# A two-layer block on one core: the last three token mixes of the second phase in one run on three row strips, and the step orders rewritten

## What is computed

```
xa = _ln(x, ln1_w, ln1_b)
sx = jnp.concatenate([state[:, 1:2] - xa[:, :1], xa[:, :-1] - xa[:, 1:]], axis=1)
xxx = jnp.tanh((xa + sx * maa_x) @ maa_w1).reshape(b, l, 5, DM)
xxx = jnp.einsum('blfd,fde->blfe', xxx, maa_w2)
xm = xa[:, :, None] + sx[:, :, None] * (maa_stack + xxx)
xk, xw, xv, xr, xg = (xm[:, :, j] for j in range(5))
w = jnp.exp(-jnp.exp(time_decay + jnp.tanh(xw @ td_w1) @ td_w2))
r, k, v = xr @ Wr.T, xk @ Wk.T, xv @ Wv.T
g = jax.nn.silu(xg @ Wg.T)
# scan over time, per head: out = r (u * k v + s);  s = k v + w * s
og = group norm of out, per head, * gn_w + gn_b
x1 = x + og * g @ Wo.T
xc = _ln(x1, ln2_w, ln2_b)
sx2 = jnp.concatenate([state[:, 0:1] - xc[:, :1], xc[:, :-1] - xc[:, 1:]], axis=1)
rr = jax.nn.sigmoid((xc + sx2 * ffn_maa_r) @ Wfr.T)
kk = jnp.square(jax.nn.relu((xc + sx2 * ffn_maa_k) @ Wfk.T))
return x1 + rr * (kk @ Wfv.T)
```

## Time and profile before

| what | value |
|---|---|
| time, median of 3 runs | 1576.75 us (1575.3 to 1579.61) |
| the profiled execution: its time, its span | 1575.7 us, 1573.9 us |
| TensorE busy | 1444.3 us, 92% |
| VectorE busy | 929.1 us, 59% |
| ScalarE busy | 719.3 us, 46% |
| GpSimd busy | 469.1 us, 30% |
| mean granted clock of TensorE | 0.967 |

### The profile page before, as it was taken

How to read it: one execution, slowest core, us unless ns; L and a number is a source line. 1 busy time by engine, 2 the same in 40 slices (tenths; PEclk the granted TensorE clock), 3 DMA queues, 4 the chain that set the end, 5 groups by cost and what they waited for, 6 DMA issues and landing times. The chain is left out here.

```text
span 1573.9 us, 33178 instructions
## 1 busy us (share of the span) xinstructions
PE 1444.3 (92%) x12352; PEld 1081.0 (69%) x12352; DVE 929.1 (59%) x2287; ACT 719.3 (46%) x1772; POOL 469.1 (30%) x530
## 2 busy tenths in 40 slices
PE   4999999999999999668899999999999999999965
PEld 4777777777777777366667667666766676767632
DVE  2444444444444443327678787878777877887651
ACT  3666666666666666412433343334433443334312
POOL 1211111111111111024334532453245334533330
PEclk9999999999999999867999999999999999999977
DMA  7431111111111100020000000000000000000000
GB/s 202 146 86 39 38 38 38 37 37 37 37 37 37 37 12 13 18 113 13 18 25 6 20 24 25 9 16 25 24 18 8 24 25 18 8 24 19 18 6 12
DMA packets 25663, 54.59 MB, mean 35 GB/s; under 512 B 3984, under 2 KB 6672, under 8 KB 24016
## 3 DMA queue, kind: packets, MB, share of 16 engines
q1 hardware_dynamic: 25552, 52.99, 11.7%
HBM read 42.23 MB, written 7.34 MB: 31 GB/s over the span
## 5 line engine op out<-in xcount | busy, mean ns | idle before, releaser
L896 POOL TENSOR_TENSOR rst<-rp,st 128x448 f32<-128x448 f32 x192 | 195.2, 1041 | 67.9 <-DVE st L1092 67.9
L268 POOL TENSOR_TENSOR aT_lo<-whole,aT_hi 128x375 fp32r<-128x375 f32 x64 | 58.6, 916 | 450.0 <-ACT whole L420 447.1
L340 DVE CUSTOM_DVE_ANT_0 probs<-a_bank,unmask 112x375 f32<-112x375 f32 x256 | 125.9, 544 | 83.1 <-PE a_bank L537 72.4
L888 POOL TENSOR_TENSOR xm<-mixed,xa 128x448 f32<-128x448 f32 x80 | 84.9, 1077 | 301.7 <-DVE mixed L1021 274.0
L439 ACT ACTIVATE probs<-probs,least 112x375 f32<-112x375 f32 x256 | 153.8, 608 | 0.0
L346 DVE RECIPROCAL inv_rows<-sums 112x128 f32<-112x128 f32 x64 | 61.0, 953 | 156.1 <-ACT probs L439 156.1
L448 ACT COPY probsT<-a_bank 125x448 f32<-125x448 f32 x192 | 90.3, 536 | 53.2 <-PE a_bank L590 53.2
L590 PEld LDWEIGHTS a_bank<-ident_sb,probs 112*125 112x125 f32 x768 | 92.0, 190 | 31.1 <-ACT keyT L430 16.3
L1100 DVE TENSOR_TENSOR rst<-rp,st 128x448 f32<-128x448 f32 x64 | 109.7, 1715 | 0.0
L590 PE MATMUL a_bank<-ident_sb,probs 112*125 112x112 f32 x768 | 100.6, 281 | 3.4 <-ACT probs L439 3.4
L1021 DVE SCALAR_TENSOR_TENSOR mixed<-b_bank,vec_sb,sx 128x112 f32<-128x112 f32 x320 | 83.0, 325 | 31.9 <-PE b_bank L1537 31.6
(11 more groups left out here) (165 smaller groups left out, 3213.5 us busy)
## 6 DMA issues: line engine op xcount, KB each, us to landing
ctx_tok<-in_ctx SPq DMA_DIRECT2D x16, 750.0 KB
xT_sb<-in_xT SPq DMA_DIRECT2D x16, 224.0 KB, 9.7
x_tok<-in_x SPq DMA_DIRECT2D x16, 224.0 KB, 9.2
x_between_layers<-x_sb SPq DMA_DIRECT2D x16, 224.0 KB, 2.3
b_x<-x_between_layers SPq DMA_DIRECT2D x16, 224.0 KB, 2.8
x_post<-x_between_layers SPq DMA_DIRECT2D x16, 224.0 KB, 2.8
out_dram<-fin SPq DMA_DIRECT2D x16, 224.0 KB, 2.3
vbd<-vtok SPq DMA_DIRECT2D x208, 16.0 KB
```

The costliest lines, as they stand in the source:

```text
L340: dve.tensor_tensor_reduce(out=probs[:, g % 2, i], in0=score_bank[i][0:T, 0:TC], in1=unmask[:, m[1]], scale=-SCALE, scalar=-LOWEST, op0=AL ...
L888: pool.tensor_tensor(xm[:, f % 2], mixed[:, f % 2], xa[:, :, 1:T + 1], ALU.add).then_inc(s_xm, 1)
L896: pool.tensor_tensor(by_chunk(rst[:, j % NPROD]), by_chunk(rp[:].rearrange("p c t -> p (c t)")), state_of(j), ALU.mult).then_inc(s_pprod, 1)
```

## The change

The rows of the gate's mix move from strip 0 to strip 1 (row 5 instead of 4), in `maa2`, in `th` and in the output of `maa_first`. Mixes k, r and g then lie on strips 0, 3 and 1 and in banks 2, 1 and 0, and TensorE computes them in one interleaved run of `maa_second`, behind `reduce 0`; before, k ran alone and r with g. The orders of all four engines' steps are rewritten:

- TensorE: `transpose_value` goes behind the gate projection and behind reductions 2 and 3, which move to that place; `reduce 1` goes behind the key projection; `attend_near 3` ahead of `project_out`; `maa_first` ahead of `ffn_receptance`.
- ScalarE: `spread_decay` goes behind the chunk keys; `decay_rate` ahead of `gn_affine`, `copy_value` behind it; `decay_factor` behind `xa_affine`; `copy_vtok` behind `tanh_gate` and `relu_square`. `tanh_gate` also waits for the decay factor now, which reads the buffer that it writes.
- VectorE: `wkv_sum` goes to the head of the step; `stats1` ahead of `finish`; `bonus_value` ahead of mixes 0 and 1; product 3 ahead of `near_values 0`; product 7 right behind mix 2; `near_values 3` and product 15 ahead of `shift2`.
- GpSimd: mix 2 stands between products 5 and 6, mix 3 behind 6, mix 4 ahead of 9, and `xa_state` ahead of 13.

SyncE's steps are as before.

```diff
 MIXES = ["maa_w", "maa_v", "maa_k", "maa_r", "maa_g"]
-MIX_ROW = [1, 2, 0, 3, 4]
+MAA_ORDER = ["maa_k", "maa_w", "maa_v", "maa_r", "maa_g"]
+LAST_ROWS = slice(MD, 2 * MD)
+MIX_ROW = [1, 2, 0, 3, 5]
...
                 act.activation(th[:, 0], pre_bank[1][:, 0:T], ACT.Tanh)
-                act.activation(th[0:MD, 1], pre_bank[1][0:MD, T:2 * T], ACT.Tanh).then_inc(s_th, 1)
+                act.activation(th[LAST_ROWS, 1], pre_bank[1][LAST_ROWS, T:2 * T], ACT.Tanh).then_inc(s_th, 1)
...
                 act.wait_ge(s_gmm, count(b, 1, 1))
+                act.wait_ge(s_wdec, count(b, 1, 1))
...
-                for o, (a, z) in enumerate(((0, P), (P, MAA * MD))):
+                for o, (a, z, rows_of) in enumerate(((0, P, slice(0, P)), (P, MAA * MD, LAST_ROWS))):
...
-                        last = pe.matmul(pre_bank[1][0:z - a, o * T:(o + 1) * T], maa1[:, c, a:z], xin[:, c], start=(c == 0),
+                        last = pe.matmul(pre_bank[1][rows_of, o * T:(o + 1) * T], maa1[:, c, a:z], xin[:, c], start=(c == 0),
...
                     attend_near(m, 1)
-                if pre:
-                    maa_second(n, (2,))
-                if scans:
                     attend_near(m, 2)
                     reduce(m, 0)
                 if pre:
-                    maa_second(n, (3, 4))
+                    maa_second(n, (2, 3, 4))
...
                 if post:
                     transpose_post(l)
                 if pre:
-                    transpose_value(n)
+                    project(n, 4, "wg", s_gmm)
                 if scans:
                     reduce(m, 2)
-                if more:
-                    transpose_x(p)
-                if pre:
-                    project(n, 4, "wg", s_gmm)
+                    reduce(m, 3)
+                if pre:
+                    transpose_value(n)
                 if post:
                     ffn_key(l)
-                    ffn_receptance(l)
                 if more:
                     maa_first(p)
                 if post:
+                    ffn_receptance(l)
                     ffn_value(l)
-                if scans:
-                    reduce(m, 3)
...
                 if pre:
+                    decay_factor(n)
                     copy_rec(n)
+                    tanh_gate(n)
+                if post:
+                    relu_square(l)
+                if pre:
                     copy_vtok(n)
-                    tanh_gate(n)
-                if post:
-                    relu_square(l)
+                if post:
                     receptance(l)
...
+                if post:
+                    wkv_sum(l)
                 if scans:
                     prefixes(m)
                     for d in range(2, CH + 1):
                         decay_key(m, d)
+                    near_products(m, 0)
                     decay_rec(m)
-                    near_products(m, 0)
                     near_products(m, 1)
+                if more:
+                    stats1(p)
                 if post and at_least(n, 3):
                     finish(later(n, -3))
-                if post:
-                    wkv_sum(l)
-                if more:
-                    stats1(p)
+                if scans:
+                    bonus_value(m)
```

More of the change, by code:

```diff
@@ L933, in step @@
                     mix(n, 1)
+                if more:
+                    rstd1(p)
                 if scan:
@@ L940, in step @@
                     gate_output(l, scan)
-                if more:
-                    rstd1(p)
                 if scan:
                     product(m, 5)
+                if pre:
+                    mix(n, 2)
+                if scan:
                     product(m, 6)
                 if pre:
-                    mix(n, 2)
                     mix(n, 3)
@@ L950, in step @@
                     product(m, 8)
-                    product(m, 9)
                 if post:
                     rstd2(l)
-                if scan:
-                    product(m, 10)
                 if pre:
@@ L958, in step @@
                 if scan:
+                    product(m, 9)
+                    product(m, 10)
                     product(m, 12)
+                if more:
+                    xa_state(p)
+                if scan:
                     product(m, 13)
                     product(m, 14)
-                if more:
-                    xa_state(p)
             run(pool, step)
@@ L1199, in step @@
                 if scans:
-                    bonus_value(m)
                     near_products(m, 2)
                     scan(m)
+                    product(m, 3)
                     near_values(m, 0)
-                    product(m, 3)
                 if post:
@@ L1207, in step @@
                 if scans:
+                    near_products(m, 3)
                     near_values(m, 1)
+                if more:
+                    apply1(p)
                 if pre:
@@ L1211, in step @@
                 if scans:
-                    near_products(m, 3)
+                    product(m, 7)
                 if pre:
                     mix(n, 3)
-                if scans:
-                    product(m, 7)
                 if post:
                     residual(l)
+                if pre:
+                    mix(n, 4)
+                if post:
+                    stats2(l)
                 if scans:
                     product(m, 11)
-                if post:
-                    stats2(l)
-                if more:
-                    apply1(p)
-                if pre:
-                    mix(n, 4)
                 if post:
@@ L1230, in step @@
                     near_values(m, 2)
+                    near_values(m, 3)
+                    product(m, 15)
                 if post:
                     shift2(l)
-                if scans:
-                    product(m, 15)
+                if more:
+                    token_shift(p)
                 if post:
@@ L1237, in step @@
                     ffn_input(l, xr2, "ffn_r", s_xr2)
-                if scans:
-                    near_values(m, 3)
+                if more:
+                    mix_input(p)
                 if pre:
                     gate(n)
-                if more:
-                    token_shift(p)
-                    mix_input(p)
                 if is_batch(l, B - 1):
@@ L1435, in step @@
                 if scans:
+                    chunk_keys_decayed(m)
+                    spread_decay(m)
                     copy_keys(m)
@@ L1446, in step @@
                 if pre:
-                    copy_value(n)
+                    decay_rate(n)
                 if post:
@@ L1450, in step @@
                 if pre:
-                    decay_rate(n)
-                    decay_factor(n)
+                    copy_value(n)
                     copy_key(n)
@@ L1458, in step @@
                 if pre:
+                    decay_factor(n)
                     copy_rec(n)
-                    copy_vtok(n)
                     tanh_gate(n)
@@ L1463, in step @@
                     relu_square(l)
+                if pre:
+                    copy_vtok(n)
+                if post:
                     receptance(l)
@@ L1678, in step @@
                 if scans:
+                    bonus(m)
                     transpose_keys(m)
-                    bonus(m)
                 if pre:
@@ L1705, in step @@
                 if pre:
-                    maa_second(n, (3, 4))
+                    maa_second(n, (2, 3, 4))
+                if scans:
+                    attend_near(m, 3)
                 if post:
                     project_out(l)
+                if pre:
+                    project(n, 2, "wk", s_kmm)
                 if scans:
                     reduce(m, 1)
-                    attend_near(m, 3)
                 if pre:
-                    project(n, 2, "wk", s_kmm)
                     project(n, 3, "wr", s_rmm)
+                if more:
+                    transpose_x(p)
                 if post:
```

13 lines of the change are left out of this document (4 added, 9 removed).

## The result

| | kernel before | kernel after |
|---|---|---|
| median of the runs | 1577.97 us (4 runs, 1575.3 to 1579.61) | 1614.51 us (4 runs, 1612.97 to 1618.83) |
| profiled execution: time, span | 1575.7, 1573.9 us | 1618.83, 1616.9 us |
| granted clock over the span | 0.967 | 0.939 |
| twelve steady steps (3 to 14) | 621.4 us, 51.8 each | 660.1 us, 55.0 each |

The changed kernel takes 1.0237 times as long (95% interval 1.0215 to 1.026), some 37 us more by the medians. Its profiled execution is the longest of its four, so the spans differ by 43.0 us; 38.6 of them lie in steps 3 to 14.

What follows compares the result with a forecast made beforehand. The prediction took a chain outside TensorE, closing through the late load of x1, to set the step: 9.6 + 3.1 + 16.9 + 23.7 + 2.0 = 55.3 us against 51.8. Twelve steps and the edges give +44 on 1575.7: 1620 us, range 1590 to 1650.

Steps and rivals of the forecast that it cites:

- the circle: Chain vtok, 13 copies, load of x1, stats1, finish, mixes, ffn_key, next vtok: sets the step at 55.3 us (52.7 to 58).
- `vtok` to the issue of the load: From vtok ready on ScalarE, through SyncE's 13 copies, to issuing the load of x1: 9.6 us.
- issue to the start of `stats1`: From SyncE's issue of the load to VectorE's stats1: landing 2.5 to 4.1 us, taken as 3.1.
- `stats1` to the three mixes: From VectorE's stats1 to TensorE's mixes: 16.9 us at the low clock, 16.0 at full clock, 14.9 without a wait.
- the mixes to the end of `ffn_key`: On TensorE, 20.0 us with reduce 3 moved in, plus 3.74 for ffn_key itself: 23.7 us.
- The wait and the clock: TensorE waits some 5 us a step ahead of gn_mean; then gn_mean (1.7 us) and chunk_sums (3.6) run at 1.2 GHz.
- The total: Twelve steps +42 us, steps 0 to 2 zero, step 15 -1, step 16 +3: +44 on 1575.7, 1620 us.
- The mixes: On TensorE one run of 1.1 us replaces 1.14 + 1.15, saving 1.06 us a step; product 7 under 2 us.
- Rival 1: The change does what it says: load in time, TensorE's 47.6 us plus 0.2 wait a step, 1524 us; chance 0.07.
- Rival 3: GpSimd's row holds VectorE's near_values, ffn_key up to 2 us late: circle 59 to 60 us, 1670 us; chance 0.09.
- The hold at the port: VectorE beside GpSimd: despite the skill's one-instruction rule, a later product can again be held through a whole GpSimd run.
- so the 2.46 us wait goes: TensorE's wait for product 7 vanishes, with reduce 1 3.6 us later and product 7 right behind mix 2.

Runs made afterwards that it cites:

- e1: Kernel after with copy_vtok moved on ScalarE to right behind tanh_gate, ahead of relu_square: 1536.7 us, ratio to before 0.9751.
- e2: Kernel after with stats1 moved on VectorE from ahead of finish to behind centre: 1540.55 us, ratio to before 0.9767.
- e3: Kernel after with SyncE's load of x1 issued one batch earlier, ahead of the 13 copies: 1542.1 us, ratio to before 0.9776.
- e4: Kernel before with only copy_vtok moved on ScalarE to behind relu_square: 1607.86 us, ratio to before 1.0194.
- e10: e6 with the gate's rows back on the first strip and the mix of k run apart from r and g: 1528.0 us, ratio to before 0.9686.
- e5: Kernel before with the gate's rows on strip 1 and mixes k, r, g in one run at the place of r and g: 1556.29 us, ratio 0.9862.
- e12: Kernel before with only the mix of k moved on TensorE to right ahead of mixes r and g, old strips kept: 1552.99 us, ratio 0.9862.
- e6: Kernel after with the edits of e1 and e3 together: 1520.25 us, ratio to before 0.9632.
- e11: Kernel before with two VectorE neighbours exchanged, product 7 ahead of the writing of mix 3: 1579.15 us, ratio 1.0007.
- e9: Kernel before with only reduce 1 moved behind the key projection: 1590.81 us, ratio to before 1.0086.

## Why the prediction was right, point by point

The forecast was 1620 us (1590 to 1650) with 0.88 on slower; it measured 1614.51. e1 to e4 show that this is for its reason: each link of the circle, taken away alone, gives all of the loss back, and one link put into before makes most of it. That the sum of the circle comes out within 0.5 us is in part luck: its terms are off by 0.2 to 0.8 us, some up and some down.

The terms of the circle against the trace of after:

| term | forecast | after |
|---|---|---|
| `vtok` to the issue of the load | 9.6 | 1143.02 to 1153.31: 10.3 |
| issue to the start of `stats1` | 3.1 | 2.7 |
| `stats1` to the three mixes | 16.9 | 1100.20 to 1116.70: 16.5 |
| the mixes to the end of `ffn_key` | 23.7 | 1116.70 to 1141.18: 24.5 |
| to the end of `vtok` | 2.0 | 1.8 |
| sum | 55.3 | 55.8 |

- *The wait and the clock.* TensorE waited 5.29 us where I had said some 5, and the clock was granted at 0.50, the 1.2 GHz level, behind it. At before's level the two multiplications take 3.03 us, not 5.01. Of these 2.0 us about 0.9 reach the circle, as the forecast's 16.9 and 16.0 had it: e1, at the full clock, has 15.65 us from `stats1` to the mixes for after's 16.5, in the step in which TensorE waits for `finish`. Windows of after, at the head-mean matmul:

```profile
1098.00:1100.00 2.00, 0.00 (x0) 0.00 (x0) 0.00 (x0) 0.00 (x0) 0.00 (x0) 0.88 0.63 213
...
1102.00:1104.00 2.00, 1.84 (x10) 0.58 (x17) 1.97 (x7) 0.00 (x0) 0.00 (x0) 0.50 0.11 30
1104.00:1106.00 2.00, 2.00 (x84) 2.00 (x92) 2.00 (x8) 0.13 (x1) 1.68 (x2) 0.50 0.27 85
```

- *The total.* Twelve steps cost 38.6 us for the 42 of the forecast: the steps average 55.0, and the one I read is at 55.5. Outside them lie 4.4 us: 1.2 up to step 3 for the 0 of the forecast, -0.6 in step 15 for -1, and 3.8 behind it for 3. In step 16 the head-mean matmul waits 3.76 us and starts 1.4 us after the last of the 13 copies is issued; the profile names no releaser, so that it waits for the copies is inferred. So terms that are too high and too low offset each other here too. The median lies 4 us under the profiled execution.
- *The mixes.* One run of 24 in 1.15 us, and product 7 at 0.61 us, as forecast. But the saving of 1.06 us a step was too large: e10 gives 7.8 us in all, or 0.7 a step in the groups, and e5 against e12 gives nothing in before's orders. I had left out that in before the mix of k runs while TensorE's next operand isn't ready: with it moved away, the packed run of e5 waits 1.56 us. This error of price didn't show in the result, since TensorE wasn't the bound.
- *Rival 1.* Its price, 1524 us with steps of 47.8, was close to what e6 reached (1520, 47.9), once its condition, a load in time, was met. The change itself doesn't meet it, as the forecast said. Its chance of 0.07 was low with cause; the change misses by a `vtok` that one line of order places.
- *Rival 3.* Its mechanism was there, its size not. I had it hold `near_values`; it was `apply2` that GpSimd's row held, and only in every second of the ten steps from 860 to 1440 us: 4.18 to 4.19 us in five, 1.40 to 1.41 in five. In the step shown it cost TensorE the 0.73 us ahead of `ffn_key`, not the 2 us of the rival. VectorE's and GpSimd's timelines of after, a held step and the one before it:

```profile
1071.06 1.40 DVE L1146 TENSOR_SCALAR ln_tok<-x,ln_mv,ln_rs 112x512 f32<-112x512 f32 x1 [0.44 <-POOL ln_rs L921]
...
1125.68 4.19 DVE L1146 TENSOR_SCALAR ln_tok<-x,ln_mv,ln_rs 112x512 f32<-112x512 f32 x1 [0.44 <-POOL ln_rs L921]
```

```profile
1071.13 1.05 POOL L890 TENSOR_TENSOR xm<-mixed,xa 128x448 f32<-128x448 f32 x1
1072.14 3.31 POOL L898 TENSOR_TENSOR rst<-rp,st 128x448 f32<-128x448 f32 x3
...
1125.75 1.05 POOL L890 TENSOR_TENSOR xm<-mixed,xa 128x448 f32<-128x448 f32 x1
1126.76 2.83 POOL L898 TENSOR_TENSOR rst<-rp,st 128x448 f32<-128x448 f32 x3
1129.53 0.39 POOL L878 COPY xa<-b_rows 128x4 f32 x1
1129.87 1.90 POOL L898 TENSOR_TENSOR rst<-rp,st 128x448 f32<-128x448 f32 x2
```

- *The hold at the port.* The earlier trace rows had product 7 held through four GpSimd instructions, and the Trainium skill (SBUF — State Buffer, Who interferes with whom) lets the engine that starts first keep the port pair for one. Here `apply2` is held through four and a small copy in one step, although it starts 0.07 us ahead of the first, and in e11 through every instruction to the end of GpSimd's row. The runs disagree with that rule as before; only the step with 1.40 us looks like a wait for one instruction.
- *What I had wrong and only the experiments showed:* that moving the reader of product 7, or product 7 itself, is enough to take out its wait. The forecast gave two grounds for "so the 2.46 us wait goes": `reduce 1` behind the key projection, and product 7 behind mix 2. e9 makes the first move alone in before and loses 14 us, e11 moves product 7 by one place and gains nothing. What the trace of after shows, product 7 at 0.61 us, fits the sentence that follows in the forecast: GpSimd waits for a mix at that place (1.41 us ahead of its sum at 1119.93), so its row is broken there. No run takes this gap alone out of after.

## What to carry to other kernels

Follow a load back to what stands ahead of it in its own queue, and that back to the engine which feeds it: a circle over ScalarE, a DMA queue and VectorE can set the step while the busiest engine's order only gets better, and a few microseconds of slack before a change are the number to hold the moved steps against. Where a VectorE instruction takes several times its length beside GpSimd, look for the gaps in GpSimd's row, and for which instruction is held: moving product 7 or its reader only moved the wait to `apply2`. The move that paid, e12, left the hold in place but on an instruction whose result nobody waits for, and put a gap where product 7 is. So look at what else is held before calling a hold gone. And price a saving on the busiest engine only after its own waits nearby are looked at, since they may already cover the work that is taken out.

## What the runs showed of the hardware

- A VectorE instruction of 0.6 to 0.9 us took 3.28 to 5.11 us in the steps shown when it was issued into a gapless row of four or more GpSimd instructions, whether the row held additions or products. In before, e9, e11 and e12 it ended within 0.5 us of the end of that row; in the held steps of after it ended with GpSimd's small copy (1129.87 us above), while the row went on with two products. It happened to `product 7` and the near product `rg` (two operand tiles) and to `apply2` (one). Yet other VectorE work runs inside such rows with at most one GpSimd instruction's delay: in e6, two of VectorE's products (one of `near_values` at 1115.67, one of `group_norm` at 1117.29) take 0.74 and 1.40 us while GpSimd runs four in a row from 1114.58 to 1119.51. And in after `apply2` starts 0.07 us ahead of the same row of GpSimd in both steps shown above, and is held in one (4.19 us) and not in the other (1.40). So a gapless row makes the hold possible, not certain; what decides is open.
- Matmuls of 32 rows on three strips: a run of 24 on three took 1.15 us interleaved and 1.69 us one run behind the other; with two of the three on one strip (e10), 2.03 us. Two on two strips take 1.15, so the third cost nothing.
- TensorE's clock was granted at 0.88 from 1098 to 1100 us in after, within its wait of 5.29 us, and at 0.50, the 1.2 GHz level, from 1100 to 1106; over 450 us in e1, whose head-mean matmul waits 1.3 us at most, it averaged 1.00. But the length of the last wait doesn't settle it. In before the clock stayed at 1.00 behind the 2.46 us (1102 to 1108 us); in e9 it fell to 0.50 behind 1.98 and 0.60; and in e12 it was 0.54 from 1136 to 1138 us, where the longest wait since the step began was 0.48, and `project_out` took 5.38 us for 3.69. What decides isn't shown here.
